# 16-head causal attention: the ban on later keys moved from TensorE's mask products into VectorE's maximum, and the stage's setting-up moved into its main block

## The reference, cut to what matters

```python
    x = x + _L0_attn_ref(_layernorm(x, axis=-1), ...)
    x = x + _L0_ffn_ref(_layernorm(x, axis=-1), ...)      # a router picks one of 8 experts a token
    x = x + _L1_attn_ref(_layernorm(x, axis=-1), L1_attn_Wqkv, L1_attn_Wo)
    x = x + _L1_ffn_ref(_layernorm(x, axis=-1), ...)      # two layers of windowed attention and MLP

def _L1_attn_ref(x, Wqkv, Wo):                            # T = 512, D = 256, H = 16, DH = 16
    qkv = x @ Wqkv.T
    q, k, v = jnp.split(qkv, 3, axis=-1)                  # then (b, H, T, DH) each
    q = cos * q + rotate_half(q) * sin
    k = cos * k + rotate_half(k) * sin
    scores = jnp.einsum('bhqd,bhkd->bhqk', q, k) / math.sqrt(DH)
    causal = jnp.tril(jnp.ones((t, t), dtype=bool))
    scores = jnp.where(causal, scores, -jnp.inf)
    attn = jax.nn.softmax(scores, axis=-1)
    out = jnp.einsum('bhqk,bhkd->bhqd', attn, v)
    return out @ Wo.T
```

## Time and profile before

| | |
|---|---|
| runs | 2721.39, 2722.84, 2726.86 us; median 2722.84 |
| profiled execution | 2726.97 us, span 2725.2 us |
| mean granted TensorE clock | 0.916 |
| busy share of the span | PE 87%, PEld (weight loads) 66%, DVE 57%, ACT 44%, POOL 35% |
| the stage `phase_attn1` | about 598 to 1232 us of the span |
| L1249, mask products | 1024 matmuls and as many weight loads |
| L1058, maxima | 384 instructions, 595 ns on the mean |
| L1718, add-and-reduce of the last stage | 512 instructions, 387 ns on the mean |

### The profile page before, as it was taken

The page is one execution under the profiler, slowest core; times in us unless marked ns, Lnnn a source line. Parts: engine busy times, 40 slices in busy tenths (PEclk is TensorE's granted clock), DMA queues, the critical chain, the costliest instruction groups (busy, mean ns, idle before and its releaser), DMA issues.

```text
span 2725.2 us, 46487 instructions
## 1 busy us (share of the span) xinstructions
PE 2377.3 (87%) x16770; PEld 1799.0 (66%) x16770; DVE 1564.7 (57%) x4242; ACT 1206.8 (44%) x3055; POOL 965.5 (35%) x1367
## 2 busy tenths in 40 slices
PE   7999699977888888886788898898888988988988
PEld 4666599965464555545567676686676766866766
DVE  5555422225647566546657558567675585585754
ACT  1112133324755555653624636437345354372362
POOL 2222122214443333323715416236155262462442
PEclk9999699987988879788899998998999989989999
DMA  3222311121010100003000000000010000000000
GB/s 123 93 100 97 106 38 36 39 71 32 3 58 7 47 18 33 2 10 111 2 16 16 17 16 1 17 16 33 16 57 16 26 8 32 16 2 32 16 2 32
DMA packets 75794, 96.31 MB, mean 35 GB/s; under 512 B 6141, under 2 KB 68946, under 8 KB 75314
## 3 DMA queue, kind: packets, MB, share of 16 engines
q1 hardware_dynamic: 70642, 81.72, 8.9%
q0 software_dynamic: 3408, 9.31, 1.2%
q10 hardware_dynamic: 1520, 2.31, 0.2%
HBM read 62.51 MB, written 30.28 MB: 34 GB/s over the span
## 4 chain that ended last, share of the span: by engine, by line
PE 30%; DVE 14%; POOL 4%; issue 3%; ACT 2%; DVEq 0%; POOLq 0%; ACTq 0%
PE l_bank L1977 6%; PE l_bank L1978 5%; PE l_bank L1979 5%; PE l_bank L2084 4%; POOL l_probs L1622 3%; DVE l_work L1699 3%; DVE l_ss L1680 2%; PE l_bank L2019 2%; PE l_turned L2037 2%; PE l_bank L2053 2%; DVE l_probs L1697 1%; DVE l_probs L1718 1%; PE l_turned L1977 1%; PE l_turned L1978 1%; PE l_turned L1979 1%
## 5 line engine op out<-in xcount | busy, mean ns | idle before, releaser
L1622 POOL TENSOR_SCALAR l_probs<-l_probs,l_rinv 128x256 f32<-128x256 f32 (+1 forms) x512 | 223.3, 455 | 129.0 <-DVE l_rinv L1723 127.9
L1058 DVE TENSOR_REDUCE c_cnmax<-cbank 128x1 f32<-128x384 f32 (+3 forms) x384 | 206.2, 595 | 108.5 <-PE cbank L1249 89.5
L1896 ACT ACTIVATE l_probs<-l_probs,l_nmax 128x256 f32<-128x256 f32 (+1 forms) x512 | 238.9, 473 | 0.0
L1158 ACT ACTIVATE c_cprobsT<-cbank 128x384 f32<-128x384 f32 (+1 forms) x384 | 180.5, 522 | 97.9 <-PE cbank L1275 97.1
L1718 DVE CUSTOM_DVE_ANT_0 l_probs<-l_bank,mask 128x256 f32<-128x256 f32 (+1 forms) x512 | 169.1, 387 | 37.3 <-PE l_bank L2019 22.8
L1606 POOL TENSOR_TENSOR l_work<-l_work 128x512 f32<-128x512 f32 x64 | 82.7, 1292 | 272.5 <-DVE l_work L1699 271.6
L979 POOL TENSOR_SCALAR_AFFINE_SELECT c_cprobsT<-c_cprobsT 128x256 f32<-128x256 f32 x256 | 99.4, 412 | 165.9 <-ACT c_cprobsT L1158 163.8
L2019 PE MATMUL l_bank<-l_kT,l_flipped 64*128 64x256 f32 (+1 forms) x1024 | 152.6, 420 | 0.0
L1942 ACT ACTIVATE l_v<-l_bank,l_b 128x512 f32<-128x512 f32 (+1 forms) x96 | 66.1, 689 | 193.0 <-PE l_bank L1979 193.0
L718 PE MATMUL h_bank<-m_xsT,m_w1s 128*128 128x128 f32 x1248 | 148.4, 278 | 0.3 <-issue 0.3
L1977 PE MATMUL l_bank<-l_part,l_w_high 128*128 128x512 f32 (+1 forms) x288 | 123.1, 427 | 26.3 <-DVE l_yT L1789 26.3
(11 more groups left out here) (273 smaller groups left out, 6358.5 us busy)
## 6 DMA issues: line engine op xcount, KB each, us to landing
w<-in_W1T SPq DMA_DIRECT2D x8, 1024.0 KB, 8.3
w<-in_W2T SPq DMA_DIRECT2D x8, 1024.0 KB, 11.3
l_came<-y_d SPq DMA_DIRECT2D x16, 512.0 KB, 4.2
ys_d<-m_y SPq DMA_DIRECT2D x39, 128.0 KB, 1.7
xn_d<-a_prods SPq DMA_DIRECT2D x8, 512.0 KB, 3.1
c_came<-x_d SPq DMA_DIRECT2D x8, 512.0 KB, 4.8
y_d<-c_raw SPq DMA_DIRECT2D x8, 512.0 KB, 3.7
y_d<-l_probs SPq DMA_DIRECT2D x8, 512.0 KB, 3.4
```

Of the source, the lines that this page charges most:

```text
L1058: dve.tensor_reduce(nmax[:, c % 2, qt, s, i:i + n], S, AX, ALU.max, negate=True).then_inc(nmax_ready[s], 1)
L1158: act.activation(probsT[s][:, c % 2, i, k0:k0 + w], turned_place(j, s)[:, 0:w], ACT.Exp).then_inc(probs_ready[s], 1)
L1622: pool.tensor_scalar(probs[s][:, held(u), h, 0:n], probs[s][:, held(u), h, 0:n], rinv[s][:, u, h:h + 1], 1.0, ALU.mult, ALU.mult)\
L1896: act.activation(probs[s][:, held(u), h, 0:n], probs[s][:, held(u), h, 0:n], ACT.Exp, bias=nmax[s][:, u, h:h + 1], scale=-1.0, accum_out=r ...
```

## The change

A table `later` of four tiles of 128 columns is added in bf16: three tiles of zeros, and the triangle of -1e30 from `g.mask`. VectorE's `row_max` uses it: in place of one reduction a unit it runs one `tensor_tensor_reduce` a head, which adds the ban to the scores, negates, takes the minimum into `nmax`, and writes the sums nobody reads into places 6 and 7 of `raw`. Since each writes over the one before, it also waits for its own stream's maximum of the unit before. TensorE's two mask matmuls a head go, and the scores' matmul closes its own group.

The first block of the stage goes: SP's loads, GpSimd's gathers and VectorE's settings stand now at the head of the same engines' lists in the main block. The waits for them are put where they are needed: VectorE waits for the first rows before its first sum and for the weights behind the first normalisation, TensorE for weights and settings behind the first transposes.

```diff
+        later = sb("later", [P, NT, P], BF16)
...
                 for s in range(NS):
                     sp.dma_start(wo[s][:], g.Wo1T[s].rearrange("(c p) n -> p c n", p=P)).then_inc(c_in, 16)
-                sp.wait_ge(first_in, 16 * NS)
-                sp.wait_ge(c_in, 64)
+                for pair in range(PAIRS):
...
                 pool.wait_ge(row_first, NS)
                 for s in range(NS):
                     gather(pool, s, 0)
-
-            @block.vector
-            def _(dve):
-                dve.tensor_copy(identr[:], g.ident[:]).then_inc(c_set, 1)
...
-                dve.memset(nmax_hl[:].bitcast(F32), 0.0).then_inc(c_set, 1)
-                dve.wait_ge(c_set, 2 + 5 * NS)
-
-        with nc.Block() as block:
...
             @block.vector
             def _(dve):
                 chain = Chain(dve, dve_chain)
+                dve.tensor_copy(identr[:], g.ident[:]).then_inc(c_set, 1)
+                dve.memset(later[:, 0:NT - 1, :], 0.0).then_inc(c_set, 1)
+                dve.tensor_copy(later[:, NT - 1, :], g.mask[:, 2, :]).then_inc(c_set, 1)
...
+                dve.wait_ge(c_set, 4 + 5 * NS)
+                dve.wait_ge(first_in, 16 * NS)
...
-                        S = score_place("scores", u, s)[:].rearrange("p (h k) -> p h k", h=n)[:, :, 0:(qt + 1) * P]
-                        dve.tensor_reduce(nmax[:, c % 2, qt, s, i:i + n], S, AX, ALU.max, negate=True).then_inc(nmax_ready[s], 1)
+                        wide = (qt + 1) * P
+                        ban = later[:, (NT - 1 - qt):NT, :].rearrange("p a b -> p (a b)")
+                        if pair * UNITS + u:
+                            dve.wait_ge(nmax_ready[s], pair * UNITS + u)
+                        for h in range(n):
+                            last = dve.tensor_tensor_reduce(raw[:, CHUNKS - NS + s, h * 2 * P:h * 2 * P + wide], score_place("scores", u, s)[:, h * 2 * P:h * 2 * P + wide], ban, -1.0, 3e38,
+                                                            ALU.add, ALU.min, nmax[:, c % 2, qt, s, i + h:i + h + 1])
+                        last.then_inc(nmax_ready[s], 1)
...
                     if pair == 0:
                         first_norm(0)
+                        dve.wait_ge(c_in, 64)
...
-                                pe.matmul(score_place("scores", u, s)[:, i * 2 * P:i * 2 * P + wide], qT[s][r, p, qt * P:(qt + 1) * P],
-                                          kT[s][r, p, 0:wide], start=True, stop=False)
-                            for half in range(2):
-                                for s in range(NS):
-                                    h = head(s, c, i0 + i)
-                                    r = slice(64 * (h % 2), 64 * (h % 2) + 64)
-                                    at = i * 2 * P + qt * P
-                                    last = pe.matmul(score_place("scores", u, s)[:, at:at + P], g.mask[r, 3 * half, :], g.mask[r, 3 * half + 2, :],
-                                                     start=False, stop=half == 1)
-                                    if half == 1 and i == n - 1:
-                                        last.then_inc(scores_ready[s], 1)
+                                last = pe.matmul(score_place("scores", u, s)[:, i * 2 * P:i * 2 * P + wide], qT[s][r, p, qt * P:(qt + 1) * P],
+                                                 kT[s][r, p, 0:wide], start=True, stop=True)
+                                if i == n - 1:
+                                    last.then_inc(scores_ready[s], 1)
...
                     if pair == 0:
                         for s in range(NS):
                             transposes(s, 0)
+                        pe.wait_ge(c_in, 64)
+                        pe.wait_ge(c_set, 4 + 5 * NS)
```

More of the change, by code:

```diff
@@ L926, in _ @@
             def _(pool):
+                for s in range(NS):
+                    pool.tensor_copy(rowb[s][:], g.row_of[:, s * NT:(s + 1) * NT]).then_inc(row_first, 1)
+                pool.wait_ge(row_first, NS)
+                for s in range(NS):
+                    gather(pool, s, 0)
                 for pair in range(PAIRS):
```

28 lines of the change are left out of this document (10 added, 18 removed).

## The result

The kernel after took 2705.34 us on the median, against 2726.53 for the kernel before beside it: ratio 0.9928, 95% interval 0.9912 to 0.9944. A second set of runs gave 0.9910 (0.9891 to 0.9928). One of the five runs of the kernel after took 3370.95 us, at a granted clock of 0.637; the ratio leaves it out. How much faster a kernel is rests on the ratios, where the time went on the traces.)

A forecast was written before the change was run, and what follows sets the result against it. TensorE, not VectorE, was taken to bound the kernel. Start -3.7, heads -4.6, half-clock masks -4.2, steady chunks -8.0 and a later clock rise +3.0 made -17.5 us: 2705.3 from the median 2722.84, range 2694 to 2722 (8 in 10).

The forecast's parts named there:

- The bound, and which masks lie on the path: Steady chunk: TensorE bounds; masks of units 1, 3 and 5 count, 0.40 us a chunk, 8.0 us in all.
- The instruction: VectorE's maxima: add-and-reduce takes 6.58 us a chunk against 6.39, covered by pauses, costing nothing on the path.
- The added wait: VectorE's wait for its own stream's maximum of the unit before: already ended by then, cost 0.
- The head: Each pair's opening scores and maxima: 1.15 us sooner, 4.6 us in all; 1.9 us beside gathers carried over unchanged.
- The start: Stage's start: without the barrier the first normalisation comes 3.7 us sooner, bounds 2 and 5.
- The clock's rise: Half-clock stretch of each pair: clock rises a fifth of a chunk later, costing 3 us in all, bounds 0 and 16.
- the first rival: Clock rises a whole chunk late in each pair, 15.6 us in place of 3, giving 2718; chance 0.17.
- masks at half clock: Stretch of 9.1 us before the clock rises: removed masks save 1.04 us a pair, 4.2 us in all.
- the second rival: Clock falls in the steady stretch or never rises, making the kernel slower, 2725 to 2781 us; chance 0.10.
- The rule weighed: TensorE cycling through PSUM banks with idle moments sees its clock go up and down; the sum did not follow it.
- Another chain takes the place: Exponent's loop and four maxima transfers end the chunk, losing the 8.0 us: 2713; chance 0.12, shared with a dearer instruction.
- The whole mask time comes off: Steady chunk: all eight mask groups count, not only those on the path, giving 2699; chance 0.06.

The follow-up runs named there:

- the repeat: Kernels before and after run once more, unchanged, on another chip than the first set of experiments: 2726.19 us before, 2699.84 us after, ratio 0.9910.
- the ban alone: Kernel before with mask matmuls replaced by VectorE's add-and-reduce, its two blocks left as they were: 2704.81 us, ratio 0.9954.
- the merged block alone: Kernel before with its first block moved into the main block, masks and reductions kept: 2718.77 us, ratio 1.0004; profiled again in a later set.
- the kernel with filled gaps: Kernel after with v products halved behind each step, ScalarE's exponents ahead of its copy, later wo loads, four maxima transfers merged into two: 2663.84 us, ratio 0.9776.

## Why the prediction was right, and where it was not

*The bound, and which masks lie on the path: right in size, one step off in place.* Forecast 0.40 a chunk, measured 0.43. Unit 1's masks gave 0.12 for 0.13, unit 3's 0.10 for 0.09. Unit 5's two groups gave 0.12 for 0.18: the two pairs of 256-column products now take 0.50 together, and without their masks they had taken 0.44 (0.23 and 0.21), so 0.06 came back. The step that I called covered by a wait for the exponent, behind unit 4, gave 0.08 for 0: in the kernel before it began 0.12 behind the last record without a wait being shown, and as everything before it moved forward, so, it seems, did its exponent. The wait at 706.53 is the rest of what was saved there. The exponent wait at 709.49 grew by 0.09 (0.42 to 0.51), as told.

*The instruction: right.* 0.61 and 0.48 from start to start, 6.58 us a chunk, covered. Two runs show the cover: with masks and ban together the chunk is 8.97, with neither 8.53. In the head I had its price in the sum; 0.27 a head is what it measures.

*The added wait: 0, right.* With the plain reduction, which has no such wait, the chunk is 0.01 shorter.

*The head: the step that failed.* "I carry that over unchanged" is wrong. The last pair gave 1.03 for 1.15; the other three gave 2.64, 2.59 and 2.37, because the gathers' hold of 1.8 to 2.1 us shrank to 0.4 to 0.5 (0 to 0.3 in the repeat). So 8.6 for 4.6. The merged block has little part in it: by itself, in a set with the hold, it had 17.3 to 17.5 where the kernel before had 17.6 to 17.9. The hold delays TensorE's signals behind some score groups. With masks, that stopped TensorE and VectorE in turn; without, VectorE works 13.54 of 15.10 us and has the next scores ready by the time. That last sentence is read from the two traces and not tested by itself. The hold also explains a part of why the ban alone gave 12.5 us in a set without it and the whole change 20 to 24 in sets with it: 4.5 to 5 us of those 7 to 12 are heads.

*The start: the landing was mis-sized.* I let stream 0's sum begin 8.0 us behind the first load (its last gather's start and 3.5 us of the earlier trace rows). It began 11.25 behind: from the start of that gather to the sum it is 6.75 us (599.01 to 605.76), where I had 3.5 from a load that stands alone. Stream 1's sum follows without a pause for its gather, 3.20 behind stream 0's (605.76 to 608.96), so "What is late next is stream 1's gather" was wrong too. The first normalisation came 17.6 us behind the start, outside the 14 to 17 that I named. 2.3 for 3.7, inside the bounds of 2 and 5; 0.3 to 1.4 of the miss go with the loads of `wo`, and the DMA engines were busy all through 596 to 602 us. The whole term could not be measured in the time of the kernel (1.0004).

*The clock's rise: a term that the runs do not show.* I expected it 8 to 11 us behind the first turned scores. It came 12.55 behind in pair 0 and 6.96, 6.74 and 7.02 in the others. But in the repeat the same kernel had 8.80, 7.34, 7.31 and 7.10, and the kernel before had 9.07, 7.20, 8.28 and 9.69 in one profile and 9.28, 7.24, 8.12 and 6.41 in the other. The means are 8.6 before and 8.3 after, and 7.8 and 7.6 in the repeat: the change did not delay the rise, and the 3.0 us of the sum stand for nothing that was measured. Pair 0 of the first profile looks like the first rival: from first turned to last scores it shrank by 1.6 us, where the others shrank by 2.9, 3.4 and 3.7. Steady chunks explain 5 x 0.43 = 2.15 of each. So masks at half clock and the rise together gave 3.1, and my two terms had made 1.2 (-4.2 and +3.0).

*What was missing: the tail, and that it trades with the stretch ahead.* No mask ran there, and it became 4.6 us longer in sum. The clock falls in it: in the kernel before 11.38, 10.11, 17.54 and 11.83 us behind the last scores, in the kernel after 9.66, 9.38, 9.18 and 9.47. A tail in which it fell 17.3 to 17.6 behind took 19.8 to 19.9 us, in all kernels with products whole; one with a fall 9.2 to 9.9 behind, 22.4 to 22.5. The first pair of the repeat and of the ban alone had the short one. In these two executions the second rival had a grain of truth: the clock was lost earlier, outside the steady stretch, for 0.2 to 2.6 us a pair. I had looked for it where TensorE is busiest and not where it was already falling. That the change makes the tails longer is not shown, though. In the repeat they grew by 0.6 and not by 4.6, and the merged block alone, masks and all, had 89.3 us of tails with falls 9.7 to 10.5 behind. The same kernel trades the two parts: in the last pair of the kernel before, one profile has a rise 9.69 behind the first turned scores, 55.9 us to the last scores and a tail of 21.6; the other has 6.41, 54.7 and 22.5. So the two rows are best read together: -7.1 in the first pair of profiles and -10.7 in the repeat, for -9.2 by the forecast.

*The rivals.* The clock never fell in a steady stretch, in none of the fourteen profiles: 1.00 over the 41.54 us above, with three waits of 0.43 to 0.51 us in each chunk. The rule weighed (the Trainium skill, "TensorE: Matmul & The Clock Gate", section "A second HAM failure mode: psum-queue depth-cycling") would have had it go up and down there; this case doesn't show it. "Another chain takes the place" was wrong for this change, and right for the next one. "The whole mask time comes off" was wrong: 0.43 of 0.72.

In sum: -17.5 forecast; -2.3 - 8.6 - 11.7 + 4.6 and +1.1 make -16.9, and the remaining 4.7 of the span's difference lie outside what the change touches, 3.9 of them ahead of the stage. The agreement of 2705.3 with 2705.34 is luck: terms that were off cancelled, and the kernel before came out at 2726.53 where the forecast had started from 2722.84, 3.7 us lower. What carried it is the mechanism and the largest term, the chunk.

## What to carry to other kernels

Write down for each step of the loop what ended its wait, and count a removed instruction only where the step was back to back; then look at the smallest slack behind it, here a transfer chain with 0.24 us left, because that is what the next improvement meets. A stall seen beside other traffic is not a constant to be carried over: it is worth as much as the chain it hits lets through. And where a clock can be lost, read the stretch in which it falls together with the one ahead of it, and over several executions: the same kernel had tails of 19.8 and of 22.5 us for the same pair. In the one profile of the kernel with filled gaps the tails gave as much as the loop itself.

## What the runs showed of the hardware

The same kernel on the same chip had heads of 15.65 us beside its gathers in one set of runs and of 17.3 to 17.5 in another; TensorE's completion signals of two groups came about 0.7 and 2.3 us late in the second. Taking the loads of `wo` from beside the gathers brought the first sum 0.3 to 1.4 us forward. Two transfers of four rows, issued in 1.26 us, did the work of four of two rows issued in 2.38, and landed early enough to end the wait. The bytes are the same, so it is the count of issues that cost; a transfer of four rows landed 1.85 us behind the start of its issue and one of two rows 1.66:

```profile
704.53 2.38 SPq L886 DMA_DIRECT2D c_cqT<-c_nmaxT  x4
```

```profile
702.38 1.26 SPq L886 DMA_DIRECT2D c_cqT<-c_nmaxT  x2
```

(the kernel after, and the merged one). And the clock: in the tail of the merged kernel TensorE was busy 13.36 of 18.04 us, 74%, and kept 1.00; in the kernel after it was busy 6.46 of 9.38, 69%, ahead of the fall, but one tail of the kernel before kept the clock for 17.54 us at 11.31 busy, 64%. The busy share ahead of the fall alone doesn't tell which tail falls early.
